# Attention: V's rows loaded at a block's fourth step and the keys of the next block but one at its second, in place of the last two steps

## What is computed

```python
# H = 16 heads of DH = 64, 4 memory keys and values ahead of the 1024 of the sequence, TOPK = 64
q, k, v = heads(x @ Wq), heads(x @ Wk), heads(x @ Wv)
k, v = concat(mem_k, k), concat(mem_v, v)
dots = einsum('bhid,bhjd->bhij', l2norm(q), l2norm(k)) * 10.0
dots = einsum('hg,bgij->bhij', W_pre_th, dots)        # mix the heads
dots = where(causal, -max, dots)
dots = where(dots < 64th largest of the row, -max, dots)
attn = einsum('hg,bgij->bhij', W_post_th, softmax(dots))
out = einsum('bhij,bhjd->bhid', attn, v) * head_scale
return (out * sigmoid(x @ Wg + bg)) @ Wo
```

## Time and profile before

| | us |
|---|---|
| median of 3 runs | 3578.09 (3574.36 to 3592.0) |
| the profiled execution: its time | 3578.9 |
| its span, first to last instruction | 3576.6 |
| outside the span | 2.3 |

### The profile page before, as it was taken

One profiled execution on the slowest core, in us unless ns is written; L12 is line 12 of the kernel. 1 busy time (PEld: TensorE's weight loads), 2 busy tenths in 40 slices (PEclk: granted clock), 3 DMA queues, 4 the chain that ended last, 5 costly groups with the idle time before them and its releaser, 6 DMA issues. The chain is left out here.

```text
span 3576.6 us, 73640 instructions
## 1 busy us (share of the span) xinstructions
PE 3147.3 (88%) x23206; PEld 2081.0 (58%) x23206; DVE 2548.2 (71%) x6406; ACT 2522.9 (71%) x5857; POOL 2020.7 (56%) x6011
## 2 busy tenths in 40 slices
PE   7999999996788998888899887899888888987998
PEld 4444444443566666755666665566676566666566
DVE  4444444434788998678999867899986889985354
ACT  3444444443788989688999967899986888995222
POOL 1221221222787767687776767776767877674332
PEclk9999999997899999989999989999997999999999
DMA  3222222225466664355666345566534556641010
GB/s 129 95 89 106 106 104 96 83 82 171 142 175 175 182 188 99 101 154 169 181 188 167 93 115 158 177 185 190 141 88 131 172 173 182 183 106 49 31 36 30
DMA packets 363531, 467.11 MB, mean 131 GB/s; under 512 B 29476, under 2 KB 295204, under 8 KB 362664
## 3 DMA queue, kind: packets, MB, share of 16 engines
q1 hardware_dynamic: 363048, 461.62, 43.8%
HBM read 227.18 MB, written 234.36 MB: 129 GB/s over the span
## 5 line engine op out<-in xcount | busy, mean ns | idle before, releaser
L1125 ACT ACTIVATE junk<-D,nt 128x76 int8<-128x76 f32 (+62 forms) x1440 | 1070.5, 747 | 96.7 <-POOL nt L1213 63.6
L1030 PE MATMUL banks<-kr,E 128*128 128x128 f32 (+1 forms) x4672 | 702.4, 299 | 115.9 <-ACT AT L1148 65.9
L1030 PEld LDWEIGHTS banks<-kr,E 128*128 128x128 f32 (+1 forms) x4672 | 602.3, 202 | 264.3 <-issue 156.0
L1003 PE MATMUL banks<-Sg,kpre 128*128 128x109 f32 (+51 forms) x1568 | 601.7, 492 | 23.3 <-POOL maskb L1282 13.1
L1355 DVE COPY Sn<-banks 128x686 f32<-128x686 f32 (+11 forms) x440 | 375.9, 854 | 167.9 <-PE banks L990 134.2
L1380 DVE SCALAR_TENSOR_TENSOR W<-SG,sgn,W 128x76 f32<-128x76 int8 (+14 forms) x480 | 412.7, 899 | 107.1 <-POOL W L1235 106.6
L989 PE MATMUL banks<-kT,qT 64*128 64x343 f32 (+11 forms) x880 | 393.1, 529 | 102.6 <-DVE Sn L1355 95.8
L1148 ACT ACTIVATE AT<-banks 128x512 f32<-128x512 f32 (+3 forms) x768 | 344.8, 479 | 187.0 <-PE banks L1030 186.2
L1058 PE MATMUL banks<-AT,V 128*64 128x64 f32 x9216 | 391.8, 233 | 82.1 <-issue 72.5
L1058 PEld LDWEIGHTS banks<-AT,V 128*64 128x64 f32 x9216 | 322.6, 142 | 156.6 <-issue 139.6
L1445 DVE SCALAR_TENSOR_TENSOR E<-D,vk,E 128x12 f32<-128x12 f32 (+56 forms) x512 | 394.5, 779 | 3.1 <-ACT E L1135 1.5
(11 more groups left out here) (197 smaller groups left out, 5250.7 us busy)
## 6 DMA issues: line engine op xcount, KB each, us to landing
score_scratch<-Sn SPq DMA_DIRECT2D x96, 343.0 KB, 3.4
v_scratch<-a_share SPq DMA_DIRECT2D x32, 512.0 KB, 3.6
q_scratch<-a_share SPq DMA_DIRECT2D x32, 512.0 KB, 2.8
k_scratch<-a_share SPq DMA_DIRECT2D x32, 512.0 KB, 2.8
gate_scratch<-a_share SPq DMA_DIRECT2D x32, 512.0 KB, 2.7
kT<-k_scratch SPq DMA_DIRECT2D x32, 512.0 KB, 5.1
gateT<-gate_scratch SPq DMA_DIRECT2D x32, 512.0 KB, 10.0
qT<-q_scratch SPq DMA_DIRECT2D x31, 512.0 KB, 6.6
```

Source lines behind the costliest of these rows:

```text
L1003: out = nc.tensor.matmul(bank[:, 0:c], kpre[:].rearrange("p h r -> p (h r)"), Sg[:, g % 3, c0:c1], start=True, stop=not diagonal)
L1030: out = nc.tensor.matmul(ps[5 + i % 2][0:rows, c % 4 * P:(c % 4 + 1) * P], E[:, g % 4, c * P:c * P + rows], kr[:, g % 4, :], start=True, s ...
L1125: nc.scalar.activation(out, D[:, e, 1:1 + n], ACT.Sign, bias=nt[:, r, e:e + 1], scale=-1.0, accum_out=cnt[:, r, e:e + 1]).then_inc(s[f"cnt ...
```

## The change

`late(G)` is split. `keep(G)` holds the two loads of V with the wait for `av`, `late(G)` the wait for the projection and the gates' load. `keep` is called at the end of step 3, and at the end of step 6 where the block is the first of a batch. `keys(G + 2)` is called at the end of step 1, and stays at the end of step 6 where block G+2 is the first of a batch. The queries stay at step 6, the gates at step 7. No instruction of another engine is edited, and each transfer keeps its shape.

```diff
-            def late(G):
+            def keep(G):
                 b, ib, r = G // IB, G % IB, G % IB * P
                 if b >= 1:
                     sp.wait_ge(s["av"], 2 * IB * b)
                 sp.dma_start(V[MEM:P, ib, :], vd[b, r:r + P - MEM, :]).then_inc(s["v_in"][G % 2], 16)
                 sp.dma_start(V[0:MEM, ib + 1, :], vd[b, r + P - MEM:r + P, :]).then_inc(s["v_in"][G % 2], 16)
+
+            def late(G):
+                b, r = G // IB, G % IB * P
                 if G >= 1:
                     sp.wait_ge(s["y"], G)
...
                 if 2 * k + 4 < NT:
                     load(2 * k + 4)
+                if G + 2 < NB and k % 8 == (1 if (G + 2) % IB else 6):
+                    keys(G + 2)
                 if k % 8 == 6 and G + 2 < NB:
-                    keys(G + 2)
                     queries(G + 2)
+                if G < NB and k % 8 == (3 if G % IB else 6):
+                    keep(G)
                 if k % 8 == 7 and G < NB:
                     late(G)
```

## The result

The changed kernel takes 3668.73 us (median of 4, 3662.69 to 3671.07) against 3577.68 (median of 4, 3574.36 to 3592.0) for the kernel before. The ratio is 1.0252, 95% interval 1.0232 to 1.0272. Slower was the likeliest of the three signs that I gave, but the size was wrong: +28 us predicted, +91 measured, and 3668.73 lies above the range's upper end of 3648. The profiled execution took 3671.07 us, with a mean granted clock of 0.931 where it was 0.947.

A forecast was written before the change was run, and what follows sets the result against it. No engine was far ahead; PE idled in step 0 waiting for V's late load, some 70 us in all. 3578.9 - 40 + 0 + 61 + 7 = 3606.9, stated as 3606 us for the median; range 3560 to 3648.

The forecast's parts named there:

- V's wait, -40: Step 0 of ib 2 to 7: PE no longer waits for V, 36 us plus 4 for ib 7, 40 us gained.
- Blocks of ib 0, nothing: V at the end of step 6: V's wait becomes one for Sg; no gain, bounds +2 and -2 us a block.
- The plug's mechanism: End of step 3: V on 4 of 16 DMA engines, 10 us flight; Sg loads and stores issued behind it land late.
- T + 12.1: Step 4: landing of the first store behind V, in us after T, the issue of the Sg load ending SP's step 3.
- The plug's price, +61: Stalls behind early V, ib 1 to 6: 19.0 us a batch, 76 in four, less a fifth: 61 us lost.
- the terms of ib 2 to 6: Stalls of PE from late stores behind early V: 5.1, 3.7, 2.2, 1 and 3.4 us a block.
- Some of it is made up afterwards: After the stalls behind early V: part of the loss is recovered, so a fifth was taken off 76 us.
- the plug costs all of it, and more: Rival: V's flight in step 3 is 11.5 us and nothing is made up, 108 us lost, 3654 us; chance 0.13.
- a flight of 7.8 us: Lower case for V's flight when issued in step 3: loss about 8 us a batch, 30 us.
- the even exchange: Rival, no change: V's flight 8.5 us, a third made up, about 35 us lost against 40 gained, 3580; chance 0.20.
- The keys, +7: Keys issued at step 1 delay what is behind them: 1.8 us a batch, 7 us lost in all, bounds 0 and 25.
- stalls in step 2 above 1 us a block: Sign that the forecast is wrong: the keys' share, 7 us, is then too small.

## Why the prediction came out as it did

**V's wait, -40: right, the number in part by luck.** Step 0 is 41.7 us shorter, and 37.5 of that in ib 2 to 6, for which I had 36. The blocks of ib 7, for which I had 4, gave nothing, and ib 1 gave 4.2. PE's idle time fell from 53.8 to 34.2 us in 15 blocks, 1.3 a block where I had 1.8. The rest of the gain, 8 us, is busy time: the granted clock of step 0 is 0.91 where it was 0.85, and the clock was not in my sum.

**Blocks of ib 0, nothing: right.** V's wait in step 0 of block 9 became one for Sg ahead of the mix, 4.34 us where I had 4.4. Block 8's last steps after:

```profile
1508.91 0.28 SPq L921 DMA_DIRECT2D V<-v_scratch  x1
...
1519.59 0.52 PE L1009 MATMUL banks<-Sg,kpre 128*128 128x149 f32 x2 [4.34 <-DMA Sg<-score_scratch]
```

The four steps 0 of ib 1 are 4.2 us shorter together, a microsecond each, within the 2 that I allowed.

**The plug's mechanism: right.** In block 10 the store lands at T + 11.7 (T = 1602.57), where I had T + 12.1. But DVE came to its wait only at T + 7.7, and so waited 3.97 us and PE 2.45, where I had 5.7 and 5.1. In block 9 PE waits 3.36 us for Sg where I had 3.6:

```profile
1545.53 0.49 SPq L921 DMA_DIRECT2D V<-v_scratch  x1
...
1555.97 1.13 PE L1009 MATMUL banks<-Sg,kpre 128*128 128x229 f32 x2 [3.36 <-DMA Sg<-score_scratch]
```

As foretold, the gates' median flight falls from 10.0 to 4.3 us (L931):

```profile
DMA to landing us min/median/max: 3.9/4.3/7.5
```

and a store's longest rises from 8.4 to 11.7 (L904):

```profile
DMA to landing us min/median/max: 2.3/3.2/11.7
```

**The plug's price, +61: this is the step that failed.** Steps 4 and 5 cost 112.0 us. The term was mis-sized because it priced a stall as idle time alone and left out the slow clock behind it. The idle time was nearly right in sum: the terms of ib 2 to 6 are 15.4 us a batch, 46 in the three batches of the 15 blocks, and PE's idle time grew by 41.0. That is partly luck, since from ib 2 to ib 6 it grew by 2.6, 2.0, 2.0, 2.4 and 4.7 us a block, where I had 5.1, 3.7, 2.2, 1 and 3.4. Behind most stalls PE works at 1.2 GHz for a while, and as PE is busy for all of step 4 this comes on top, 27.5 us in the same 15 blocks. In all 24 blocks of ib 1 to 6 the stretches cut at the same matmuls are 106 us longer: 66 idle, where I had 76 and took off a fifth, and 40 busy, where I had nothing. "Some of it is made up afterwards" was thus true of the idle time at most; what came afterwards was more loss. A check is ib 1: steps 4 and 5 of blocks 9 and 25 ran at 0.50 in both kernels, so they had no clock to lose. Step 5 of block 9 before:

```profile
1532.43:1539.12 6.69, 6.69 (x50) 5.43 (x48) 3.68 (x19) 5.03 (x21) 5.43 (x23) 0.50 0.15 43
```

and after:

```profile
1549.60:1560.02 10.42, 7.06 (x50) 5.51 (x48) 3.70 (x19) 5.06 (x21) 5.42 (x24) 0.50 0.24 77
```

It is 3.7 us longer, 3.36 of them idle, and I had 3.6. That the slow clock is the stall's doing was tested, not only read: V in pieces at the same place takes the stalls away, and the same instructions need 317.6 us again instead of 343.9. By the length of steps 4 and 5, ib 2 (7.2 us a block against 5.1) and ib 6 (6.9 against 3.4) were furthest off.

The strongest rival, "the plug costs all of it, and more" (3654), came nearest, but for another reason: it took a longer flight, and the flight was as forecast. Two side sums were loose without touching the forecast: by its own terms a flight of 7.8 us costs 7 us a batch and not 8, and the even exchange loses 28 us and not 35.

**The keys, +7: too small by a factor of nearly four.** 26 us alone, just outside my bound of 25, and 19.7 in step 2 of the changed kernel. The stall of 1.4 us that I had worked out for ib 1 did not come: with the keys alone, steps 1 and 2 of its four blocks are 1.1 us longer together. I had half a microsecond for ib 2 and 3 and room elsewhere; measured in step 2, with the keys alone, are 6.6, 6.0, 3.4 and 3.7 us in four blocks each of ib 2 to 5, 0.9 to 1.7 a block. The stores behind the keys were late: DVE waited 20.8 us for them instead of 5.4. I looked at the next use of Sg and not at the stores in step 2. The sign that I had named for this ("stalls in step 2 above 1 us a block") shows in the changed kernel: its step 2 is 0.9 to 1.5 us a block longer in ib 2 to 5.

**What the rows already held.** The better change could be read from the trace of before: a share of 0.25 while V was alone says that V itself is slow, and I took that as a given, where it was the thing to mend.

Left open: whether V's early load in pieces would gain if `Sn` had a third part, so that a late store holds nobody. It wasn't tried.

## What to carry to other kernels

A transfer that uses 4 of 16 DMA engines delayed the stores and loads issued behind it here, from either of two queues; look at the DMA share while it is alone, and cut its partitions (here 112 + 12 for 124) before moving it. Moving a slow transfer away from its wait moves the wait: price it by who uses what is issued behind it, stores that free a buffer too. Where TensorE is busy throughout, price a stall at more than its own length: here 41.0 us of idle time brought 27.5 us more of busy time at the slow clock. And when a stretch of two runs is compared, cut it at the same instructions of the engine in question; cut at another engine's steps, it mixes in work of the step before.

## What was not expected of the hardware

- The granted clock fell from 1.00 to 0.50 behind 2.4 us of idling in block 10, and stood there from 1616 to past 1619. In 15 blocks the slow clock made 27.5 us of busy time to 41.0 us of idle time, and in three of them it did not fall at all. The Trainium skill, page "TensorE: Matmul & The Clock Gate", section "What's actually happening", describes two levels that depend on how busy PE has recently been; by that, the trace agrees.
- One cut of a load, 124 partitions into 112 and 12, was worth 1.4% of the kernel at the old place, and 2.6% (3668.7 to 3571.7) in the changed kernel.
- Issuing the keys in 124 + 4 partitions held the issuing engine for 6.90 us. V has 124 partitions too, in runs of 4 KB instead of 512 bytes, and its issue takes 0.49. The two differ in the number of runs, 8 to 1; that this is the cause was not tested by itself.
